# Local attention: head pairs in the halves of the array, four steps, V products last, 192 keys

## The reference, cut to what matters

```
def _layer(x, wqkv, qs, ksc, wo, ...):
    h = shift_token(x)
    q, k, v = split(h @ wqkv, 3)              # 8 heads of 64
    q = l2norm(q) * qs;  k = l2norm(k) * ksc
    q, k = rotary_xpos(q, k)                  # t*cos*scale + rotate_half(t)*sin*scale
    o = local_attention(q, k, v)
    x = x + o @ wo
    ...                                       # then a gated feed-forward
def local_attention(q, k, v):                 # windows of 64 tokens, each sees itself and the one before
    sim = einsum(q * 8, k)
    mask = (i < j) | (i > j + 64)
    return softmax(where(mask, -big, sim)) @ v
```

## Time and profile before

| | |
|---|---|
| median of three runs | 2102.8 us (2099.29 to 2106.86) |
| the profiled execution, its own time | 2104.7 us |
| its span (first to last instruction) | 2102.9 us |
| PE busy | 1732.1 us, 82% of the span |
| DVE, ACT, POOL busy | 1334.4, 1084.2, 541.9 us |
| local attention, layer 0: first maxima to last inversion of sums | 1219.4 to 1392.7 us |
| the same in layer 1, last inversion | 1665.9 us |
| inversions of the sums, start to start | 22.4 us in the steady batches |

### The profile page before, as it was taken

One profiled execution on the slowest core, in us unless ns is written; L12 is line 12 of the kernel. 1 busy time (PEld: TensorE's weight loads), 2 busy tenths in 40 slices (PEclk: granted clock), 3 DMA queues, 4 the chain that ended last, 5 costly groups with the idle time before them and its releaser, 6 DMA issues. The chain is left out here.

```text
span 2102.9 us, 34161 instructions
## 1 busy us (share of the span) xinstructions
PE 1732.1 (82%) x10923; PEld 908.2 (43%) x10923; DVE 1334.4 (63%) x3440; ACT 1084.2 (52%) x2290; POOL 541.9 (26%) x600
## 2 busy tenths in 40 slices
PE   6747999943699999999999489977799775899933
PEld 4412333312455455455555356653566531333312
DVE  5546676646555556555657579854789637677746
ACT  3302666648444445554554277744677430667633
POOL 0036546110200000000000376602676105333000
PEclk9866999975899999999999799989899985899965
DMA  4033222000200000000000000000000003212000
GB/s 139 11 70 92 74 70 71 17 18 0 67 1 6 7 1 6 7 1 6 6 6 1 22 1 0 0 11 21 1 0 0 11 8 61 68 43 45 18 11 20
DMA packets 60002, 53.58 MB, mean 25 GB/s; under 512 B 9797, under 2 KB 52297, under 8 KB 59473
## 3 DMA queue, kind: packets, MB, share of 16 engines
q1 hardware_dynamic: 58128, 50.93, 9.5%
q10 hardware_dynamic: 1728, 0.79, 0.3%
HBM read 30.96 MB, written 1.05 MB: 15 GB/s over the span
## 5 line engine op out<-in xcount | busy, mean ns | idle before, releaser
L771 DVE CUSTOM_DVE_ANT_0 minus_s_l2x<-s_ps_l2x,mask_b_l2x 128x512 f32<-128x512 f32 x256 | 166.9, 689 | 222.8 <-PE s_ps_l2x L942 222.7
L848 ACT ACTIVATE probs_l2x<-minus_s_l2x,nmax_l2x 128x512 f32<-128x512 f32 x256 | 182.6, 714 | 213.7 <-DVE nmax_l2x L771 213.7
L1314 DVE CUSTOM_DVE_ANT_0 junk_l1x<-s_ps_l1x,mask_b_l1x 128x512 f32<-128x512 f32 x256 | 166.4, 688 | 95.6 <-PE s_ps_l1x L1516 94.1
L1317 DVE TENSOR_REDUCE nmax_l3x<-s_ps_l3x 128x1 f32<-128x512 f32 x256 | 163.3, 685 | 66.4 <-PE s_ps_l3x L1516 64.7
L1377 ACT ACTIVATE pT_l1x<-st_ps_l1x 128x1024 f32<-128x1024 f32 x128 | 131.2, 1025 | 72.9 <-PE st_ps_l1x L1504 72.5
L792 DVE COPY pT_l2x<-t_ps_l2x 128x512 f32<-128x512 f32 x256 | 164.3, 683 | 0.5 <-PE t_ps_l2x L982 0.5
L2174 ACT ACTIVATE probs_l2a<-minus_s_l2a,nmax_l2a 128x128 f32<-128x128 f32 (+1 forms) x256 | 113.9, 447 | 91.2 <-DVE nmax_l2a L2077 89.3
L714 POOL TENSOR_TENSOR inv_parts_l2x<-inv_l2x,nothing_l2x 128x32 bf16<-128x32 f32 x9 | 2.3, 253 | 593.0 <-DVE inv_l2x L763 593.0
L982 PEld LDWEIGHTS t_ps_l2x<-consts,probs_l2x 128*128 128x128 f32 x1024 | 110.8, 142 | 98.0 <-issue 88.0
L942 PE MATMUL s_ps_l2x<-kT_l2x,q_l2x 64*128 64x512 f32 x512 | 145.5, 645 | 8.0 <-issue 4.9
L1377 ACT ACTIVATE pT_l3x<-st_ps_l3x 128x1024 f32<-128x1024 f32 x128 | 130.1, 1022 | 37.4 <-PE st_ps_l3x L1504 35.8
(11 more groups left out here) (460 smaller groups left out, 3607.0 us busy)
## 6 DMA issues: line engine op xcount, KB each, us to landing
kT_l1x<-parts_l1x SPq DMA_DIRECT2D x96, 64.0 KB
kT_l3x<-parts_l3x SPq DMA_DIRECT2D x96, 64.0 KB
mask_i_l1x<-in_mask SPq DMA_DIRECT2D x8, 512.0 KB, 4.0
maskT_i_l1x<-in_mask_t SPq DMA_DIRECT2D x8, 512.0 KB, 4.8
q_l1x<-parts_l1x SPq DMA_DIRECT2D x84, 32.0 KB
q_l3x<-parts_l3x SPq DMA_DIRECT2D x84, 32.0 KB
ctxT_l2x<-in_ctxT SPq DMA_DIRECT2D x10, 256.0 KB, 2.7
ctxT_l0x<-in_ctxT SPq DMA_DIRECT2D x9, 256.0 KB, 3.0
```

What stands on the lines that cost most here:

```text
L771: dve.tensor_tensor_reduce(out=minus_s[n % (2 * DEEP)][:], in0=s_ps[n % DEEP][:], in1=mask_b[u][:], scale=-1.0, scalar=3e38, op0=ALU.add, ...
L848: act.activation(probs[n % (2 * DEEP)][:], minus_s[n % (2 * DEEP)][:], ACT.Exp, bias=nmax[:, u, n:n + 1], scale=-1.0, accum_out=sums[:, u, ...
L1314: dve.tensor_tensor_reduce(out=junk[w][:], in0=s_ps[w][:], in1=mask_b[b % 2][:, j, :], scale=-1.0, scalar=3e38, op0=ALU.add, op1=ALU.min, ...
L1317: dve.tensor_reduce(to, s_ps[w][:], AX.X, ALU.max, negate=True).then_inc(m.s_drained[w].sem, 1)
```

## The change

- Scores are taken for a pair of heads at once: head 2g on rows 0 to 63 and head 2g + 1 on rows 64 to 127 of the array, each into its own bank. q is stored per pair like k, so its drain is one ScalarE copy and its memset to zero goes.
- Query tile 1 is taken against keys 64 to 255, 192 instead of 256. The columns 128 to 191 of the probabilities are set to zero once and still transposed.
- A batch has four steps of a pair instead of eight of a head. In a step TensorE runs the scores of the next pair, six transposes and the fills of `due`, the V product last. ScalarE copies the second head's transposed probabilities, ahead of its exponentials; VectorE the first head's.
- `due` is written out by hand, and with it `order`; LAST and SUMS come in step 0, SUMS ahead of LAST.
- The norm chain goes tile by tile: VectorE does normalise(b + 1, tile 1) in step 0, the sums and own part of tile 0 of b + 2 in step 1, its normalise in step 2, sums and own part of tile 1 in step 3. POOL's power of tile 0 comes ahead of other_half of tile 1. Ahead of the loop tile 0 of batch 1 is normalised too.
- `invert_sums` comes first in step 0, ahead of the maxima.

```diff
-    TILES = (slice(0, P), slice(P, BAND))
+    TILES = (slice(0, P), slice(P + 64, BAND))
...
-    after = {QK: 1, QK + 1: 1, QK + 2: 2, QK + 3: 2, LAST: 1, SUMS: 2, TURN: 1, TURN + 1: 3, TURN + 2: 3, TURN + 3: 4, SPREAD: 5,
-             SPREAD + 1: 5, V: 4, V + 1: 6, OUT: 6}
-    after.update({GROUP + g: 2 * g + 3 for g in range(NG - 1)})
...
+    due = [[QK, QK + 1, SUMS, LAST],
+           [QK + 2, TURN, TURN + 1, TURN + 2, TURN + 3, GROUP],
+           [SPREAD, SPREAD + 1, QK + 3, V, GROUP + 1],
+           [V + 1, OUT, GROUP + 2]]
+    order = sum(due, [])
...
                         for w in range(1 if isinstance(b, int) and b == 0 else 2):
                             pool.wait_ge(*ring.empty(*at(QK + 2 * j + w)))
                             other_half(pool, j, w)
-                    for j in range(TPB):
                         cols = slice(j * 2 * NH, (j + 1) * 2 * NH)
...
                     for j in range(TPB):
                         sum_squares(b, j)
                         own_part(b, j, at)
-                    if b == 0:
-                        for j in range(TPB):
+                        if b == 0:
                             other_half(dve, j, 1)
+                        if (b, j) != (1, 1):
                             normalise(b, j)
...
+                    for s in range(STEPS):
+                        if s == 0:
                             invert_sums(b, u)
+                        if s + 1 < STEPS or left >= 1:
+                            maxima(*ahead(i, u, s + 1))
+                        dve.wait_ge(*ring.full(*group_before(i, u, s)))
+                        dve.wait_ge(*m.turned.after(NH * b + 2 * s + 1))
+                        dve.tensor_copy(pT[s % 2][:, 0].rearrange("p c t -> p (c t)"), t_ps[0][:, 0:BAND]).then_inc(m.unit_copied[0].sem, 1)
+                        if s == 0 and left >= 1:
+                            normalise(b + 1, 1)
+                        if s == 1 and left >= 2:
+                            sum_squares(b + 2, 0)
+                            own_part(b + 2, 0, at)
+                        if s == 2:
+                            for f in range(SPREAD, OUT):
+                                drain(i, u, f, turn(i, u, f))
+                            if left >= 2:
+                                normalise(b + 2, 0)
+                        if s == 3:
+                            if left >= 2:
+                                sum_squares(b + 2, 1)
+                                own_part(b + 2, 1, at)
+                            drain(i, u, OUT, turn(i, u, OUT))
...
-                        act.activation(q[1 - u][0:HD, 0:NH:2, cols], bank[0:HD], ACT.Copy)
-                        act.activation(q[1 - u][HD:P, 1:NH:2, cols], bank[HD:P], ACT.Copy).then_inc(ring.drains(*at[1:]), 1)
+                        act.activation(q[1 - u][:, :, cols], ring.bank(*at[1:])[:].rearrange("p (g t) -> p g t", t=P), ACT.Copy)\
+                            .then_inc(ring.drains(*at[1:]), 1)
...
+                    for s in range(STEPS):
+                        act.wait_ge(*ring.full(*group_before(i, u, s)))
+                        act.wait_ge(*m.turned.after(NH * b + 2 * s + 2))
+                        act.activation(pT[s % 2][:, 1].rearrange("p c t -> p (c t)"), t_ps[1][:, 0:BAND], ACT.Copy).then_inc(m.unit_copied[1].sem, 1)
+                        if s + 1 < STEPS or left >= 1:
+                            exponentials(*ahead(i, u, s + 1))
+                        for f in due[s]:
...
                             drain(i, u, f, turn(i, u, f), unused=f < (LAST, TURN, 0)[left])
...
+                    halves = [(s_ps[hh], slice(HD * hh, HD * (hh + 1))) for hh in range(2)]
+                    for out, rows in halves:
+                        pe.matmul(out[:, 0:P], q[u][rows, g, 0:P], kT[u][rows, g, 0:P], start=True, stop=True)
+                    for out, rows in halves:
+                        pe.matmul(out[:, TILES[1]], q[u][rows, g, P:S], kT[u][rows, g, 64:S], start=True, stop=True).then_inc(m.scores_ready.sem, 1)
...
+                    for s in range(STEPS):
+                        if s + 1 == STEPS and left >= 1:
                             for f in range(TURN, V):
                                 pe.wait_ge(*ring.empty(*turn(i, u, f)))
+                        if s + 1 < STEPS or left >= 1:
+                            pe.wait_ge(*m.max_ready.after(TPB * (NH * b + 2 * s + 2)))
+                            scores(*ahead(i, u, s + 1))
+                        pe.wait_ge(*m.probs_ready.after(TPB * (NH * b + 2 * s + 2)))
+                        for n in (2 * s, 2 * s + 1):
+                            pe.wait_ge(*m.unit_copied[n % 2].after(STEPS * b + s))
+                            for c in range(3):
+                                ins = pe.transpose(t_ps[n % 2][:, c * P:(c + 1) * P], probs[n % (2 * DEEP)][:, c * P:(c + 1) * P], k["ident"])
+                            ins.then_inc(m.turned.sem, 1)
+                        for f in due[s]:
                             fill(i, u, f, turn(i, u, f), unused=f < (LAST, TURN, 0)[left])
```

More of the change, by code:

```diff
@@ L2025, in normalise @@
                 def normalise(b, j):
[L2027 to L2028 removed]
+                    dve.wait_ge(*m.step.after(CHAIN * b + 3 * j + 2))
                     if isinstance(b, int) and b == 0:
@@ L2085, in attend @@
                     at = lambda f: turn(i, u, f)
-                    for n in range(DEEP, NH + DEEP):
-                        c = n - DEEP
-                        if n < NH or left >= 1:
-                            maxima(*ahead(i, u, n))
-                        if c % 2 == 0:
-                            dve.wait_ge(*ring.full(*group_before(i, u, c // 2)))
-                        dve.wait_ge(*m.turned.after(NH * b + c + 1))
-                        dve.tensor_copy(pT[c // 2 % 2][:, c % 2].rearrange("p c t -> p (c t)"), t_ps[c % 2][:, 0:BAND])\
-                            .then_inc(m.turned_copied.sem, 1)
-                        if c in SUMMED and left >= 2:
-                            sum_squares(b + 2, SUMMED.index(c))
-                        for f in due[c]:
-                            drain(i, u, f, turn(i, u, f))
-                        if c == 0:
-                            invert_sums(b, u)
-                        if c < TPB and left >= 1:
-                            normalise(b + 1, c)
-                        if c in OWN and left >= 2:
-                            own_part(b + 2, OWN.index(c), at)
+                    for s in range(STEPS):
+                        if s == 0:
+                            invert_sums(b, u)
+                        if s + 1 < STEPS or left >= 1:
[18 more added lines that the diff above has]
+                            drain(i, u, OUT, turn(i, u, OUT))
@@ L2178, in _, with exponentials @@
-                for n in range(DEEP):
-                    exponentials(0, 0, n)
+                def exponentials(i, u, g):
+                    for n in (2 * g, 2 * g + 1):
+                        for j, cols in enumerate(TILES):
+                            act.wait_ge(*m.max_ready.after(TPB * (NH * (2 * i + u) + n) + j + 1))
+                            act.activation(probs[n % (2 * DEEP)][:, cols], minus_s[n % (2 * DEEP)][:, cols], ACT.Exp,
+                                           bias=nmax[:, u, TPB * n + j:TPB * n + j + 1], scale=-1.0,
+                                           accum_out=sums[:, u, j, n:n + 1]).then_inc(m.probs_ready.sem, 1)
@@ L2180, in attend @@
+                exponentials(0, 0, 0)
                 def attend(i, u, left=2):
                     b = 2 * i + u
-                    for n in range(DEEP, NH + DEEP):
-                        if n < NH or left >= 1:
-                            exponentials(*ahead(i, u, n))
-                        for f in due[n - DEEP]:
-                            drain(i, u, f, turn(i, u, f), unused=f < (LAST, TURN, 0)[left])
-                        if n - DEEP in SQUARED and left >= 2:
-                            square(b + 2, SQUARED.index(n - DEEP), lambda f: turn(i, u, f))
@@ L2269, in fill @@
                         of, g = (1 - u, NG - 1) if f == LAST else (u, f - GROUP)
-                        pe.wait_ge(*m.turned_copied.after(NH * b + (0 if f == LAST else 2 * (g + 1))))
+                        for copied in m.unit_copied:
+                            pe.wait_ge(*copied.after(STEPS * b + (0 if f == LAST else g + 1)))
                         pe.wait_ge(*ring.free(*at))
@@ L2292, in _ @@
                     pe.wait_ge(*ring.empty(*prepared(0, f)))
-                for n in range(DEEP):
-                    scores(0, 0, n)
+                scores(0, 0, 0)
                 pe.wait_ge(*m.ready_made.after(8))
```

81 lines of the change are left out of this document (29 added, 52 removed).

## The result

The kernel after takes 2125.6 us, median of four runs (2123.61 to 2125.77), against 2102.7 us (2099.29 to 2106.86) before: ratio 1.0106, 95% interval 1.0086 to 1.0125. It is slower, and the forecast of 2103 (2083 to 2116) missed it. The span of the profiled execution is 2123.6 us against 2102.9.

The account below looks back on a forecast made before the run. TensorE bounds it before; after, a closed chain through SUMS and VectorE, 22.3 us a round. Per layer 6.4 + 6 x 22.3 + 29.0 + 3.8 = 173.0 against 173.4; two layers -0.8: 2103 us (2083 to 2116).

Parts of the forecast that it names:

- the paragraph on the clock: TensorE behind the SUMS wait: a fall to 1.2 GHz costs 1.2 us, in one batch of four, + 0.3 a round.
- rival 2: The SUMS wait drops TensorE to 1.2 GHz in every batch: round 23.2 us, total 2113 us; chance 0.18.
- VectorE's end to SUMS: End of a round: from the end of VectorE's normalise through POOL's split to the next SUMS, 0.35 us.
- VectorE's stretch: VectorE from step 2's maxima to step 0's normalise, without a pause: 13.65 us of the round.
- The prologue: Ahead of the loop: the added normalise of batch 1's tile 0 delays the first maxima by 3.8 us, 2.4 to 5.
- TensorE's pair of scores: Scores of two heads on 64 rows each: 0.75 us (0.68 to 0.95), against 1.30 before, saving 2.2 us a batch.
- Rival 3: The array's two halves take turns: 1.1 + 0.1 us a pair, round 22.9 to 23.2, total 2112 us; chance 0.10.
- The chain: SUMS waits for POOL's split behind normalise, scores wait behind SUMS: a closed round of 22.0 us, 21.4 to 23.1.
- The power: POOL's power of tile 1 in the norm chain: 2.9 us at the median, just in time for normalise's multiplication.
- Rival 1: Split slips in early or the TURN+3 wait hides, no closed chain: round 20.5 us, total 2081 us; chance 0.34.
- Batch 7: Last batch of a layer, bare: 3.3 us a step, 13.5 us to the inversion, before 11.98.
- About 18.6 us of TensorE work remain: TensorE's work left in a batch after the edit saves 2.2 us on the score pairs.

Follow-up runs that it names:

- e3: Kernel after with two more 512-column products of useless work in the SUMS fill ahead of its wait: 2113.5 us, 1.0068 of before.
- e5: e2 with scores on whole rows again, q padded with zeros and drained in halves: 2096.4 us, 0.9986 of before.
- e1: Kernel after with SUMS moved from step 0 to step 1, behind TURN+3 and ahead of GROUP: 2080.0 us, 0.9899 of before.
- e2: Kernel after with the inversion moved to step 3 and POOL's split of the inverted sums ahead of its power of tile 1: 2073.6 us, 0.9883 of before.
- e4: Kernel after with POOL multiplying in place of the power -0.5, leaving out the norms' scaling: 2068.6 us, 0.9851 of before.
- e6: e2 with query tile 1 against all 256 keys again: 2084.4 us, 0.993 of before.
- e9: Kernel after with the V products first instead of last in their steps: 2111.6 us, 1.005 of before.
- e10: e2 with the V products first instead of last in their steps: 2080.9 us, 0.991 of before.
- e8: e2 with batch 0 in the old order ahead of the loop and first maxima before batch 1's tile 0 is normalised: 2070.4 us, 0.9867 of before.

## Why the prediction was wrong

**The step that failed** is the paragraph on the clock: "I take 1.2, and let it happen in one batch of four: + 0.3". It happened in every steady batch and cost 1.5 us a round (e3). That is rival 2, to which I had given 0.18; its 2113 us is too low as well, for it put a round at 23.2 and a steady one takes 23.4 to 24.1. I had the row for it, a 2.54 us wait ahead of a fall, and had worked out a wait of 2.3; I judged a difference of 0.2 us as if a wait just under the only known case were safe. The wait came out at 2.6 to 3.0, because two small terms of the same chain were too small: VectorE's end to SUMS (0.8 us for 0.35) and VectorE's stretch (13.8 for 13.65). By e3 a steady round has 22.3 us of chain for the 22.0 forecast, and 1.5 us of clock for 0.3. Six rounds take 143.0 us in layer 0 and 141.5 in layer 1, for the 133.8 of six times 22.3.

**The prologue** is the second miss, a mis-sized term: + 3.8 us, "not over + 5", is + 8.1 and + 7.6. From batch 1's sums to the maxima it is 1213.97 to 1223.99, 10.0 us for 5.6 before, where I had 9.1. The larger part of the miss lies in batch 0, which I had put at 0.4: from the first QK fill to batch 1's sums it takes 27.4 us for 23.8. POOL, which takes the power of tile 0 now ahead of other_half of tile 1, keeps VectorE waiting (timeline of both, kernel after):

```profile
1191.86 3.81 POOL L1972 TENSOR_TENSOR rn_l2a<-ssc_l2a,consts 128x16 f32<-128x16 f32 x1 [2.06 <-DVE ssc_l2a L2012]
1195.64 1.39 POOL L1922 TENSOR_TENSOR other_l2a<-qk_l2a,tb_l2a 128x256 f32<-128x256 f32 x2
...
1197.14 1.23 DVE L2031 TENSOR_TENSOR own_l2a<-own_l2a,other_l2a 128x1024 f32<-128x1024 f32 x1 [3.54 <-POOL other_l2a L1922]
```

VectorE wants an addition that needs only tile 0, but the semaphore that it waits on counts tile 1's first half with it: the wait in the code asks for 2 x TPB + 2 (j + 1) rotations. POOL's reordering was a row of the diff, and I had followed VectorE's order through the prologue and not POOL's.

**Sum of the misses.** Layer 0: rounds 9.2, prologue 4.2, last two batches 0.6, 14.0 us; layer 1: 7.7, 3.8, 1.0, 12.5 us. The rest of the program gave 5.1 back. The forecast span, 2102.9 - 0.8, with 14.0 + 12.5 - 5.1 is 2123.5; measured 2123.6.

Point by point, the rest of the steps:

- TensorE's pair of scores: 0.75 us forecast, 0.75 measured; in e5 a pair on whole rows with 192 columns takes 1.20, and TensorE's work 1.65 us a batch more. Rival 3 (halves take turns, 1.2 us a pair) is refuted by the 0.75.
- The chain: right. SUMS, LAST, scores, transposes, ScalarE, TURN + 3, GROUP, scores, VectorE, split. e1, e2 and e4 each cut it at another link and each gives steady rounds of 19.7 to 20.4 us; e3 leaves it closed and gives 22.3. In pieces: SUMS to the transposes' end 4.0 us for 2.5 (the clock); from there to the scores of step 3 4.3 for 4.4; VectorE's stretch 13.8 for 13.65; its end to SUMS 0.8 for 0.35.
- VectorE's end to SUMS: the first split operation starts only as the power ends, 1346.57, and the second lies beside the multiplication. I had two of the four behind it in 0.35 us; they and the handover take 0.8.
- The power: I took 2.9 us, the median; in three steady batches of this kernel seven take 3.86 on average. The multiplication still doesn't wait for it, as forecast (it ends at 1346.57, the multiplication starts at 1346.98). Whether a power of 2.9 us would have helped is not shown: it would have ended at 1345.7, as the addition starts (1345.64), and beside an addition the first split operation took 1.07 us. e4, with 1.13 us there, has the split done before the addition.
- What goes with the longer power is the same in all the traces: VectorE's own_part, begun ahead of it (no run changes that alone). Apart from e4, the 285 powers that start while own_part is running take 3.80 to 3.94 us, the other 67 take 2.89 to 3.17, though own_part or an addition begins within most of these too. Timeline of both, kernel before, then after:

```profile
1309.84 2.90 POOL L1974 TENSOR_TENSOR rn_l2a<-ssc_l2a,consts 128x16 f32<-128x16 f32 x1 [4.21 <-DVE ssc_l2a L2014]
1310.34 1.22 DVE L2022 TENSOR_TENSOR own_l2a<-qk_l2a,ta_l2a 128x1024 f32<-128x1024 f32 x1
```

```profile
1342.62 1.23 DVE L2020 TENSOR_TENSOR own_l2a<-qk_l2a,ta_l2a 128x1024 f32<-128x1024 f32 x1
1342.77 3.83 POOL L1972 TENSOR_TENSOR rn_l2a<-ssc_l2a,consts 128x16 f32<-128x16 f32 x1 [2.28 <-DVE ssc_l2a L2012]
```

- The Trainium skill (SBUF — State Buffer, Who interferes with whom) has a VectorE instruction with two SBUF inputs contend with a GpSimd instruction that reads SBUF. The trace agrees: the second split operation takes 1.27 us beside the multiplication, and in e2 0.22 us beside a reduction, which has one input.
- Rival 1 (no closed chain, 2081): it is not what this kernel does, but its size was right: with the chain open a batch is 19.7 to 20.4 us, and the kernel 2069 to 2080.
- Batch 7: 13.5 forecast, 13.7 measured. Batch 6 is 21.2 with a wait of 4.3 us at SUMS, which the forecast didn't name as such.
- Two figures of the prediction don't follow from their terms. "About 18.6 us of TensorE work remain" should be 64.4 / 3 - 2.2 = 19.3; e2's window has 18.8. And 6.4 us from the first maxima to SUMS has named terms of only 5.4 (1.0, 0.15, 1.0, 0.47, 2.4, 0.35); the kernel took 6.5, so that term was right by luck, or by a step that is not written down.

Not settled: why batch 0's QK fills and all behind them stand up to 8 us apart between kernels that share that code.

## What to carry to other kernels

When an in-order queue gets a fill that waits for a slow helper engine, price the wait by what stands behind it: here one fill's place (e1) or the helper's order of two jobs (e2) was worth 46 to 52 us, where going back to whole rows and to 256 keys costs 22.7 and 10.7 in the open kernel (e5, e6). Treat a new TensorE wait near the length of one after which the clock has fallen as a likely fall in every round, not in some, and give it its price in the forecast. And walk the prologue for every engine whose order changes.

## What the runs showed of the hardware

- Waits of TensorE at SUMS and the clock behind them, over both layers: 0.8 to 1.2 us (e3) and 1.4 to 1.7 us (e9), ten steady batches each, no fall; 2.6 to 3.0 us (after, ten steady batches) and 2.6 to 4.3 us (batch 6 of after, e3 and e9), each with a fall to 1.2 GHz. Before, the waits of 2.54 and 2.55 us in batch 6 of the two layers, each with a fall.
- Outside the steady batches the length of the wait alone does not decide. In batch 7 of e10 a wait of 2.00 us stands ahead of a fall; ahead of the loop in e8 (layer 0) one of 2.94 us has no fall for 3.5 us behind it. Timeline of TensorE, and windows behind the wait, e10 and then e8:

```profile
1374.16 0.49 PE L2291 MATMUL s_ps_l2a<-kT_l2a,q_l2a 64*128 64x128 f32 x4 [2.00 <-ACTq L2131]
1375.00:1378.40 3.40, 3.40 (x17) 2.20 (x18) 1.54 (x9) 1.89 (x8) 0.00 (x0) 0.50 0.01 2
```

```profile
1218.49 0.49 PE L2298 MATMUL s_ps_l2a<-kT_l2a,q_l2a 64*128 64x128 f32 x4 [2.94 <-DVE nmax_l2a L2074]
1218.40:1222.00 3.60, 3.22 (x18) 1.81 (x18) 2.84 (x5) 1.55 (x7) 3.60 (x3) 1.00 0.00 0
```

- A wait of 1.3 us ahead of the last OUT fill of a layer has a fall behind it in both layers of before and in layer 0 of after, and none in layer 1 of after and both layers of e2. So no run here gives a length up to which a wait is safe.
- The fall can be cheaper to prevent than to bear: 1.7 us of useless products a batch made the kernel 12 us faster (e3 against after).
- POOL's 16-column operations are very uneven: 0.22 us alone or beside a reduction or maxima, 0.36 at the end of VectorE's addition, 1.27 beside its multiplication; the power 2.9 us at the median before, 3.8 at the median after, by which of the power and own_part begins first.
